# A feature-crossing tower on one core: embedding stores by quarter tile, full-size tower matmuls, the last tile's layers in single pieces

## The reference, cut to what matters

```python
e = stack([tbl_f[ids[:, f]] for f in range(32)], axis=1)     # (1024, 32 fields, 32 dims)
z = einsum('bhd,bmd->bhmd', e, e).reshape(b, 32 * 32, k)
x1 = einsum('bpd,pj->bjd', z, W0)                            # (1024, 128, 32)
z = einsum('bhd,bmd->bhmd', e, x1).reshape(b, 32 * 128, k)
x2 = einsum('bpd,pj->bjd', z, W1)
h = concatenate([sum(concatenate([x1, x2], axis=1), axis=-1), dense_ctx], axis=1)   # 256 + 16
h = maximum(h @ W_top1 + b_top1, 0.0)                        # 272 -> 512
h = maximum(h @ W_top2 + b_top2, 0.0)                        # 512 -> 256
y = h @ W_top3                                               # 256 -> 1
```

## Time and profile before

| what | us |
|---|---|
| median of 3 runs (lowest, highest) | 489.16 (488.78, 489.78) |
| the profiled execution's own time | 488.35 |
| its span in the profile | 486.5 |
| PE busy in the span | 425.9 |
| PEld busy | 326.0 |
| DVE busy | 313.3 |
| POOL busy | 310.0 |
| ACT busy | 255.2 |

### The profile page before, as it was taken

One profiled execution on the slowest core, in us unless ns is written; L12 is line 12 of the kernel. 1 busy time (PEld: TensorE's weight loads), 2 busy tenths in 40 slices (PEclk: granted clock), 3 DMA queues, 4 the chain that ended last, 5 costly groups with the idle time before them and its releaser, 6 DMA issues.

```text
span 486.5 us, 6903 instructions
## 1 busy us (share of the span) xinstructions
PE 425.9 (88%) x2400; PEld 326.0 (67%) x2400; DVE 313.3 (64%) x329; ACT 255.2 (52%) x450; POOL 310.0 (64%) x262
## 2 busy tenths in 40 slices
PE   0005849599999999999999999999999999999986
PEld 0002537378777877778777877787778876787785
DVE  5005669495778765985498568866698549855500
ACT  1002737383486447574577348634866467734621
POOL 6777778777877787778788787777778710000000
PEclk9999979799999999999999999999999999999999
DMA  7449596979596969595979797949586877700000
GB/s 221 125 108 260 135 242 164 262 198 268 149 294 181 272 146 258 117 256 163 227 180 229 180 247 205 275 119 276 157 246 171 194 191 200 169 0 1 0 1 1
DMA packets 54482, 86.24 MB, mean 177 GB/s; under 512 B 10184, under 2 KB 14992, under 8 KB 54448
## 3 DMA queue, kind: packets, MB, share of 16 engines
q1 hardware_dynamic: 46256, 81.59, 58.8%
q0 software_dynamic: 8192, 4.21, 8.4%
HBM read 79.47 MB, written 6.30 MB: 176 GB/s over the span
## 4 chain that ended last, share of the span: by engine, by line
PE 79%; POOL 11%; DMA 4%; issue 4%; ACT 1%; SPq 1%; DVE 0%
PE XO L433 20%; PE WA L478 12%; PE U L469 11%; POOL emb L255 11%; PE XO L440 6%; PE XO L437 5%; PE XO L436 5%; PE U L449 5%; PE M L489 4%; PE M L498 3%; PE XO L442 3%; PE M L490 3%; DMA fac<-scratch 1%; DMA scratch<-emb 1%; PE WA L458 1%
## 5 line engine op out<-in xcount | busy, mean ns | idle before, releaser
L255 POOL DMA_INDIRECT emb<-in_table,rows x256 | 309.3, 1208 | 80.4 <-issue 77.7
L433 PE MATMUL XO<-z,w0f 128*128 128x512 f32 x256 | 123.7, 606 | 40.2 <-DVE z L380 40.2
L399 DVE TENSOR_TENSOR zl<-ZS,zh 128x1024 fp32r<-128x1024 f32 x64 | 78.1, 1221 | 74.5 <-ACT zh L262 74.3
L380 DVE TENSOR_TENSOR z<-fac 128x1024 f32<-128x1024 f32 x64 | 77.7, 1214 | 63.8 <-DMA fac<-scratch 48.4
L262 ACT ACTIVATE zh<-ZS 128x1024 fp32r<-128x1024 f32 x64 | 66.1, 1033 | 67.8 <-DVE ZS L388 67.8
L433 PEld LDWEIGHTS XO<-z,w0f 128*128 128x128 f32 x256 | 44.4, 194 | 73.8 <-issue 72.9
L388 DVE TENSOR_TENSOR ZS<-fac 128x1024 f32<-128x1024 f32 x64 | 78.3, 1223 | 1.1
L436 PE MATMUL XO<-zh,w0h 128*128 128x512 f32 x128 | 76.2, 596 | 0.0
L469 PE MATMUL U<-eblk,x1t 128*128 128x128 f32 x512 | 69.2, 279 | 1.0 <-ACT G L262 1.0
L262 ACT ACTIVATE G<-U 128x512 f32<-128x512 f32 x64 | 38.7, 605 | 59.4 <-PE WA L478 52.2
L262 ACT ACTIVATE eblk<-WA 32x512 f32<-32x512 f32 x64 | 37.6, 588 | 60.8 <-PE WA L458 59.7
(11 more groups left out here) (38 smaller groups left out, 309.3 us busy)
## 6 DMA issues: line engine op xcount, KB each, us to landing
fac<-scratch SPq DMA_DIRECT2D x256, 256.0 KB
emb<-in_table,rows POOLq DMA_INDIRECT x256
scratch<-emb SPq DMA_DIRECT2D x16, 256.0 KB
b<-scratch SPq DMA_DIRECT2D x64, 64.0 KB, 5.9
scratch<-emb SPq DMA_DIRECT2D x16, 128.0 KB
wt<-in_W_top SPq DMA_DIRECT2D x2, 512.0 KB, 8.7
z<-in_W_pairs SPq DMA_DIRECT2D x2, 256.0 KB, 2.7
idc<-in_ids SPq DMA_DIRECT2D x1, 128.0 KB, 2.0
```

The costliest lines, as they stand in the source:

```text
L255: eng.indirect_dma_start(emb[par][:, g, :], None, table, bass.IndirectOffsetOnAxis(rows[:, k, g:g + 1], 0))\
L380: eng.tensor_tensor(z[i % ZB][:, :, :], equal, fac[s][:, 2:4, :], ALU.mult).then_inc(z_done, 1)
L399: eng.tensor_tensor(zl[i % 2][:, :, :], ZS[:, :, :], zh[i % 2][:, :, :].bitcast(F32), ALU.subtract)\
L433: eng.matmul(o, w0f[:, t, :], zb[:, t, :], start=(t == 0), stop=False)
```

## The change

**Units.** A tile is split in 4 units (UNITS) of 8 gathers instead of 2 halves of 16. A unit is 2 chunks (PER). SP stores a unit when its 8 gathers have landed, and the loads of its 2 chunks wait for that store. The two DMAs of a store write runs of 256 floats (URUN) instead of 512. In the scratch the columns lie in the order of the chunks, so a load reads 512 consecutive columns of a row, as before. `emb_transposes` and `eblk_copy` also go by units: 2 transposes and 4 copies of half the columns, each unit one step later than its first chunk. The places where chunk n lands in G and zf follow from `chunk_at`.

**Full-size matmuls.** `wt1d` and `dT` get 128 partitions, zero from 16 on; W_top3's two columns are the first column of `wt3`, two zeroed 128 x 128 weights. VectorE zeroes the three tiles at the start (`tower_zero`), and SP loads `wt1d` and `dT` after that.

**Last tile.** The fixed lags hold for tiles 0 to 6. Tile 7 has `last_tile`: the part of hidden layer 1 that needs only x1 and the dense features goes ahead of `x2_products`; the four pieces lie in four PSUM banks, each released singly, with the relu alternating between ScalarE and VectorE; hidden layer 2 goes through its input pieces as they come; the two result matmuls go one by one. The product for chunk 62 goes to a bank of ZS (`g_bank`), so that it needn't wait for the copy of chunk 61 out of U1.

```diff
-    RUN = COLS // NQ
-    HALVES = 2
-    HG = P // NQ // HALVES
...
+    UNITS = 4
+    PER = CHUNKS // UNITS
+    UG = P // NQ // UNITS
+    WIDTH = UG // NQ
+    URUN = UG * D
...
-        wt1d = sb("wt1d", [ND, H1])
+        wt1d = sb("wt1d", [P, H1])
         wt2 = sb("wt2", [P, N1, H2])
-        dT = sb("dT", [ND, B])
+        dT = sb("dT", [P, B])
         vec = sb("vec", [P, N1 + 2 * N2])
+        wt3 = sb("wt3", [P, N2, P])
...
-        LAST = CHUNKS * (TILES - 1) + Y_AT + 1
-
-        def place(n, start=0):
-
-            half, s = divmod(n, NQ)
-            at = start + P // NQ * s + BC * half
-            return slice(at, at + BC)
+        END = TILES - 1
+
+        def chunk_at(n):
+
+            unit, x = divmod(n, PER)
+            return slice(PER * x, PER * x + PER), slice(UG * unit, UG * unit + UG)
 
         def tile_at(i, lag):
 
             k, n = divmod(i - lag, CHUNKS)
-            return k if n == 0 and 0 <= k < TILES else None
+            return k if n == 0 and 0 <= k < END else None
+
+        def g_bank(i):
+
+            return ZS[:, 1, :] if i == TOTAL - 2 else U1[:, :]
+
+
+        L1_BANKS = (M[:, 0, :], XO[0][:, 0:P], U0[:, 0:P], XO[1][:, 0:P])
+        L2_BANKS = (ZS[:, 0, 0:P], ZS[:, 1, 0:P])
+        Y_BANK = U1[:, 0:P]
...
+            eng.wait_ge(tower_zero, 3)
+            eng.dma_start(wt1d[0:ND, :], w_top1[KT1 * P:KT1 * P + ND, :]).then_inc(tower_loaded, 16)
+            eng.dma_start(dT[0:ND, :], dense_t).then_inc(tower_loaded, 16)
+
+            def store(k, unit):
 
 
                 par = k % 2
-                eng.wait_ge(gathered[par][half], 16 * HG * (k // 2 + 1))
-                for row, n in ((0, P), (F, NQ * DUPS)):
-                    dst = bass.AP(scratch.tensor, scratch.offset + (k * ROWS + row) * COLS + BANK * half,
-                                  [[RUN, n], [1, BANK]])
-                    eng.dma_start(dst, emb[par][0:n, HG * half:HG * half + HG, :].rearrange("p g d -> p (g d)"))\
-                       .then_inc(stored[half], 16)
+                eng.wait_ge(gathered[par][unit], 16 * UG * (k // 2 + 1))
+                for row, n in ((0, F), (F, DUPS)):
+                    dst = bass.AP(scratch.tensor, scratch.offset + (k * ROWS + row) * COLS + NQ * URUN * unit,
+                                  [[COLS, n], [URUN, NQ], [1, URUN]])
+                    eng.dma_start(dst, emb[par][0:NQ * n, UG * unit:UG * unit + UG, :].rearrange("p g d -> p (g d)"))\
+                       .then_inc(stored[unit], 16)
 
             def load(k, n):
                 i = CHUNKS * k + n
-                half, s = divmod(n, NQ)
-                at = scratch.offset + k * ROWS * COLS + RUN * s + BANK * half
-                if s == 0:
-                    eng.wait_ge(stored[half], STORES * (k + 1))
+                at = scratch.offset + k * ROWS * COLS + BANK * n
+                if n % PER == 0:
+                    eng.wait_ge(stored[n // PER], STORES * (k + 1))
...
-                if i + EARLY < TOTAL and (i + EARLY) % NQ == 0:
-                    j = (i + EARLY) // NQ
-                    store(j // HALVES, j % HALVES)
+                if i + EARLY < TOTAL and (i + EARLY) % PER == 0:
+                    store(*divmod((i + EARLY) // PER, UNITS))
...
+            def eblk_copy(k, unit):
+
+                eng.wait_ge(et_made, UNITS * k + unit + 1)
+                wait(eng, g_made, CHUNKS * (k - 1) + PER * (unit + 1))
+                many = WIDTH * NQ
+                for v in range(NQ):
                     r = slice(F * v, F * v + F)
-                    copy(eblk[r, 16 * half:16 * half + 16, v, :].rearrange("p (g s) h -> p g s h", s=NQ),
-                         WA[r, :].rearrange("p (g h s) -> p g s h", g=NQ, s=NQ)).then_inc(eblk_made, 1)
+                    copy(eblk[r, many * unit:many * unit + many, v, :].rearrange("p (g s) h -> p g s h", s=NQ),
+                         WA[r, 0:WIDTH * P].rearrange("p (g h s) -> p g s h", g=WIDTH, s=NQ)).then_inc(eblk_made, 1)
...
+            x2_copy(END)
+            for c in range(0, N1, 2):
+                eng.wait_ge(l1_made, END + c + 1)
+                eng.activation(h1[:, c, :], L1_BANKS[c], ACT.Relu, bias=vec[:, c:c + 1]).then_inc(l1_kept, 1)
+            eng.wait_ge(l2_made, END + 1)
+            eng.activation(h2[:, 0, :], L2_BANKS[0], ACT.Relu, bias=vec[:, N1:N1 + 1]).then_inc(l2_kept, 1)
+            eng.wait_ge(y_made, END + 1)
+            eng.wait_ge(y_stored[END % 2], 16 * (END // 2))
+            copy(y[END % 2][:, :], Y_BANK[0:1, :]).then_inc(y_kept, 1)
...
+            for part in (wt1d[:, :], dT[:, :], wt3[:, :, :]):
+                eng.memset(part, 0.0).then_inc(tower_zero, 1)
...
+            eng.wait_ge(l2_made, END)
+            for c in range(1, N1, 2):
+                eng.wait_ge(l1_made, END + c + 1)
+                eng.tensor_scalar(h1[:, c, :], L1_BANKS[c], vec[:, c:c + 1], 0.0, ALU.add, ALU.max).then_inc(l1_also, 1)
+            eng.wait_ge(y_made, END)
+            eng.wait_ge(l2_made, END + 2)
+            eng.tensor_scalar(h2[:, 1, :], L2_BANKS[1], vec[:, N1 + 1:N1 + 2], 0.0, ALU.add, ALU.max).then_inc(l2_also, 1)
...
+                if i == TOTAL - 2:
+                    eng.wait_ge(zl_done, TOTAL)
...
-                    w = N1 + N2 + a
-                    m = eng.matmul(M[0:1, 0, :], vec[:, w:w + 1], h2[:, a, :], start=(a == 0), stop=(a == N2 - 1))
+                    m = eng.matmul(M[:, 0, :], wt3[:, a, :], h2[:, a, :], start=(a == 0), stop=(a == N2 - 1))
...
+            def last_tile():
+
+                rows = slice(P * END, P * END + P)
+                eng.wait_ge(summed, TOTAL)
+                eng.wait_ge(x1_kept, TOTAL)
+                eng.wait_ge(xt_kept, TOTAL)
+                eng.wait_ge(y_kept, END)
+                for a in range(N1):
+                    cols = slice(P * a, P * a + P)
+                    eng.matmul(L1_BANKS[a], wt1[:, 0, cols], zf[:, 0, rows], start=True, stop=False)
+                    eng.matmul(L1_BANKS[a], wt1d[:, cols], dT[:, rows], start=False, stop=False)
+                x2_products(END)
+                eng.wait_ge(x2_kept, TILES)
+                for a in range(N1):
+                    cols = slice(P * a, P * a + P)
+                    eng.matmul(L1_BANKS[a], wt1[:, 1, cols], zf[:, 1, rows], start=False, stop=True).then_inc(l1_made, 1)
+                for c in range(N1):
+                    if c % 2 == 0:
+                        eng.wait_ge(l1_kept, N1 * END + c // 2 + 1)
+                    else:
+                        eng.wait_ge(l1_also, c // 2 + 1)
+                    for a in range(N2):
+                        m = eng.matmul(L2_BANKS[a], wt2[:, c, P * a:P * a + P], h1[:, c, :], start=(c == 0), stop=(c == N1 - 1))
+                        if c == N1 - 1:
+                            m.then_inc(l2_made, 1)
+                eng.wait_ge(l2_kept, N2 * END + 1)
+                eng.matmul(Y_BANK, wt3[:, 0, :], h2[:, 0, :], start=True, stop=False)
+                eng.wait_ge(l2_also, 1)
+                eng.matmul(Y_BANK, wt3[:, 1, :], h2[:, 1, :], start=False, stop=True).then_inc(y_made, 1)
...
-                if i < TOTAL and i % NQ == 0:
-                    emb_transposes(*divmod(i // NQ, HALVES))
+                if 0 <= i - 1 < TOTAL and (i - 1) % PER == 0:
+                    emb_transposes(*divmod((i - 1) // PER, UNITS))
```

More of the change, by code:

```diff
@@ L115, in dlrm_cin_tower @@
         eblk_zero = sem("eblk_zero")
+        tower_zero = sem("tower_zero")
+        wt3_made = sem("wt3_made")
         rows_made = sem("rows_made")
-        gathered = [[sem(f"gathered{i}{j}") for j in range(HALVES)] for i in range(2)]
-        stored = [sem(f"stored{j}") for j in range(HALVES)]
+        gathered = [[sem(f"gathered{i}{j}") for j in range(UNITS)] for i in range(2)]
+        stored = [sem(f"stored{j}") for j in range(UNITS)]
         et_made = sem("et_made")
@@ L246, in _ @@
                 par = k % 2
-                for half in range(HALVES):
+                for unit in range(UNITS):
                     if k > 1:
-                        eng.wait_ge(stored[half], STORES * (k - 1))
-                        eng.wait_ge(et_made, HALVES * (k - 2) + half + 1)
-                    for g in range(HG * half, HG * half + HG):
+                        eng.wait_ge(stored[unit], STORES * (k - 1))
+                        eng.wait_ge(et_made, UNITS * (k - 2) + unit + 1)
+                    for g in range(UG * unit, UG * unit + UG):
                         if g % GROUP == 0:
@@ L328, in _ @@
             eng.wait_ge(tower_loaded, 16 * 5)
+            copy(wt3[:, :, 0], vec[:, N1 + N2:]).then_inc(wt3_made, 1)
             eng.wait_ge(eblk_zero, 1)
-            for i in range(-1, LAST + 1):
+            for i in range(-1, TOTAL + 3):
                 if 0 <= i - 1 < TOTAL:
@@ L340, in _ @@
                         z16_high((i + 1) // 2)
[L341 to L344, removed]
                 if tile_at(i, X2_AT + 1) is not None:
```

(24 more changed lines are left out.)

30 lines of the change are left out of this document (16 added, 14 removed).

## The result

The changed kernel takes 495.10 us (median of 4, 493.44 to 495.81) against 488.97 for the kernel before on the same chip: a ratio of 1.0138, 95% interval 1.0109 to 1.0166. It is 1.4% slower, where 459.3 and faster was forecast. The profiled execution took 493.44 us, its span is 491.6, 5.1 more than before.

What follows compares the result with a forecast made beforehand. TensorE was taken as the bound at 52.2 us per tile, with data short at the start. Start 11, matmuls 12.6 and tail 6.2 sum to 29.8 off 488.35, giving 458.55, or 459.3 as median; range 454.5 to 467.

Steps and rivals of the forecast that it cites:

- What the units add: Costs of smaller units: sixteen more stores, their landings, eblk copies and start zeroing; all put at nothing on the path.
- the ring of five chunks: In steady work it covers the added stores and landings, as SP has some 20 us of TensorE work in hand.
- At most its 6.4 us: Bound on each unit's cost in SP's queue if the cover went: one store landing under load.
- The start, 11 us: Tile 0: earlier store, VectorE's z near 29, chunk 10's products at 96.6 against 108.02; 17 us from gather to z.
- The zeroing, put at nothing: At the start VectorE zeroes 1,792 columns before anything waits for it, idling 28 us ahead of 38.84; cost nothing.
- Full-size matmuls, 12.6 us: Hidden layer 1 and result matmuls without 0.19 us size changes: 1.80 us less per tile, tiles 0 to 6.
- row count doesn't matter: Rival: the 0.19 us belongs to changes of tile or bank and stays; 472 us, chance 0.05.
- The tail, 6.2 us: Last tile: 0.5 us saved ahead of x2_products, 5.7 behind it; between 5 and 7 in all.
- Nothing on the path: ScalarE's eight further, half-sized eblk copies per tile, each at most 0.6 us, leave it under 36.4 of 50.4 us.
- The gathers: GpSimd's gathers at 1.25, then 1.51 us each: the 48th ends at 73.0, the 80th at 121.3, feeding TensorE.
- Their rival for the slower side: Gathers slowed by VectorE's denser work become the bound; beyond 1.72 us each 490 and up, chance 0.03 for slower.
- The store's size: Stores write 1 KB runs for 2 KB; any cost lies inside the bounds of the 17 us from gather to z.

Runs made afterwards that it cites:

- run 9: Changed kernel with each store from the 5th unit on put one chunk of loads earlier in SP's queue; 465.7 against 488.3 us, ratio 0.956.
- run 14: Kernel before with the units of 8 gathers alone, thin matmuls and old tail kept; 501.9 against 488.4 us, ratio 1.027.
- run 13: Kernel before with the full-size matmuls alone; 474.6 against 488.4 us, ratio 0.973.
- run 8: Changed kernel with 2 units of 16 gathers per tile instead of 4 of 8; 471.3 us, ratio 0.967 to the kernel before.
- run 5: Changed kernel with the stores of two units standing together, ahead of four chunks' loads, from tile 1 on; 470.6 against 488.1 us, ratio 0.962.
- run 6: Changed kernel with each store from the 7th unit on put two chunks of loads earlier; 472.0 us, ratio 0.968 to the kernel before.
- run 7: Changed kernel whose loads from tile 1 on read the tile before in the scratch, without waiting for their own store; 466.5 against 488.3 us, ratio 0.957.
- run 15: Changed kernel with every store but the first put one chunk of loads earlier, also in tile 0; 468.8 against 488.4 us, ratio 0.960.
- the repeats: Second measurements of six versions, on chips where the kernel before took 488.1 to 488.4 us; they took 466.5 to 501.9 us.

## Why the prediction was wrong, point by point

- **The step that failed** is in "What the units add": the landings "are covered by the ring of five chunks". The ring covers a late load, a delay that comes once; it doesn't cover a period. What had to be summed is the cycle of SP's queue per unit. From the fifth store on it is, on the mean, 6.7 us for two chunks of loads, 1.8 for the store and 4.9 until the next load goes, 13.5 us with the gaps, where TensorE needs 12.6. The store's two DMAs were taken at 0.9 us. The ring only put off the effect by a tile or two. "At most its 6.4 us" per unit was right as a bound (the pauses are 1.4 to 6.3 us), but what a unit cost is the excess of the cycle: the six periods took 322.0 us where 302.4 were forecast, 0.8 us for each of 24 units. No rival had it.
- **Where the 34.9 us went.** The span was forecast at 486.5 - 29.8 = 456.7 and came at 491.6. Of the difference, 12.5 are the start, 19.6 the six periods, 2.0 the stretch between the last two x2_products, and 0.8 the end behind them.
- **The start, 11 us:** -1.5 came. The first z went at 30.77, near the 29 forecast, so the early start itself is real. The sentence "SP has nothing else behind them that could go" was wrong: behind the waiting SP stand the next unit's loads, and behind these the next store. From the 48th gather's end to z of chunk 10 it took 73.3 to 103.1, 29.8 us, where 17 were taken and 20.3 was the far end. With the store moved up (run 9) tile 0's x2_products start 7.6 us before those of the kernel before. The sign of the -1.5 isn't shown: with the units alone (run 14) they start at 110.1, and with two units at 110.3 (run 13) and 114.0 (run 8), where the kernel before has 112.5.
- **The zeroing, put at nothing,** holds up the gathers. The third gather, before and after, beside VectorE's zeroing of eblk:

```profile
4.62 3.47 DVE L360 MEMSET eblk<- 128x4096 f32 x1 [0.80 <-issue]
6.76 2.69 POOL L255 DMA_INDIRECT emb<-in_table,rows  x1 [0.31 <-issue]
9.76 0.95 POOL L255 DMA_INDIRECT emb<-in_table,rows  x1 [0.30 <-issue]
```

```profile
6.43 3.47 DVE L389 MEMSET eblk<- 128x4096 f32 x1 [0.80 <-issue]
6.68 4.58 POOL L272 DMA_INDIRECT emb<-in_table,rows  x1 [0.30 <-issue]
11.56 0.94 POOL L272 DMA_INDIRECT emb<-in_table,rows  x1 [0.30 <-issue]
```

  In both the third gather ends 1.36 us after that zeroing. The three new zeroings stand in front of it, so the fourth gather starts at 11.56 for 9.76, and near there in runs 5 to 9, 13 and 15, which have them (11.53 to 11.65), but not in run 14, which has none (9.67). The gathers behind it, up to the 20th, come 1.8 us later too. No run shows what this costs in the end.
- **Full-size matmuls, 12.6 us:** right. 50.4 us per tile in the repeats wherever TensorE is full, and 13.8 us in all by run 13, which has the last tile too. The rival "row count doesn't matter" is refuted by run 13. Not every change of the row count costs something, though: the 96-row matmul at the end of a chunk's products takes 0.23 us in the chain (at 461.95 in the kernel before), as the 128-row ones ahead of it do, and the four transposes behind it take the plain 0.44. The Trainium skill, "TensorEngine Tiling (Array Packing)", section "Key Properties", says that a change of the tiling mode drains TensorE; the 0.19 us at each change between 16 and 128 rows, gone in run 13, agree with it, but no run shows that the 16 rows are such a mode.
- **The tail, 6.2 us:** 4.9 of 5.7 came behind x2_products (4.7 us to the end of the last copy, for 9.55). Ahead of them 0.5 and a tile's 1.8 were due, and 0.3 came. The timeline after says why:

```profile
471.85 0.78 ACT L279 ACTIVATE eblk<-WA 32x256 f32<-32x256 f32 x2
...
472.65 0.27 ACT L279 ACTIVATE y<-M 1x128 f32<-1x128 f32 x1
472.82 0.57 ACT L279 ACTIVATE x<-XO 128x512 f32<-128x512 f32 x1
...
474.01 0.63 PE L488 MATMUL U<-ident,x 128*128 128x128 f32 x4 [1.67 <-ACT x1t L279]
...
478.11 7.31 PE L521 MATMUL WA<-G,w1s 128*128 128x128 f32 x64
...
489.82 0.27 ACT L279 ACTIVATE y<-U 1x128 f32<-1x128 f32 x1 [0.86 <-PE U L579]
```

  ScalarE has the last unit's copies to eblk and the copy of y in front of the copy of chunk 63's x1 (x, at 472.82), and TensorE's transposes of chunk 63 wait 1.67 us, by the profile for the copy of x1t behind it. With two units (run 8) the stretch between the last two x2_products is 40.4 us; in the repeats that have four units and the new last tile it is 42.1. "Nothing on the path" held for the steady tiles, not there.
- **The gathers** came close: the 48th ends at 73.3 (forecast 73.0) and the 80th at 120.1 (121.3). For the 48th that is partly luck: the gathers began 1.8 us later, and from the 20th on went at 1.46 us instead of 1.51. Their rival for the slower side was the wrong one: a queue in front of TensorE became the bound, but SP's, not GpSimd's.
- **The store's size:** what it costs was said to be within the 17 us. Size didn't decide it: runs 5, 6 and 9 have the small stores and are faster. The place did, directly behind the loads.

Left open: why SP's cycle is near 12 us in the period of tile 0 (140.6 to 152.9 between two stores) and 13.6 to 16.3 between 219 and 309 us. The store's issue takes 1.4 to 3.5 us there, mostly over 2, in place of 1.25, but no run tells why.

## What to carry to other kernels

Where one in-order queue issues a write, waits for it to land and then issues the reads, sum the queue's own cycle (issue times, plus the landing behind whatever is in flight) and hold it against the period of the bound engine; buffers ahead of it cover a late item, not a longer cycle. Halving the piece doubles how often the wait is paid, and makes it longer where the queue no longer pauses ahead of the write: 4.5 us each here, where SP used to wait for gathers first and then 2.6. The same change is 1.4% slower with the wait directly behind each store and 4.4% faster with one chunk of loads in between. Read a wait's price under load, not from its first, idle occurrence (2.1 us). And work that an idle engine does at the start is not free before one has looked at what runs beside it: here VectorE's zeroing held up GpSimd's gathers by 1.8 us.

## What was not expected of the hardware

A store issued right behind 2 MB of loads lands 5.5 us after its issue (233.91 + 2.15 to 241.55), against 2.1 us for the first, twice as large, store of the kernel before, ahead of all loads. A change between 16-row and 128-row matmuls costs 0.19 us, and is gone with zero padding (run 13); a change between 96 and 128 rows costs nothing that shows. A gather issued beside VectorE's zeroing of eblk ends 1.36 us after the zeroing and takes 2.69 or 4.58 us for it, where the two ahead of it and those behind it take about 1.
